# A hybrid block in one launch: two pairs of stages joined, expert weights kept in SBUF, residual rows loaded through ScalarE's queue

## The chip, the cores and the metric

The kernel runs on one core of a Trainium2 chip. The metric is the device time of one execution in microseconds, the median of several. The profile is of one execution.

## The reference

The input x has 2 x 2048 rows of 256 features. Four layers follow, each added to x:

```python
x = x + attn_a(layernorm(x), ...)   # neural memory
x = x + ffn(layernorm(x), ...)      # product-key memory
x = x + attn_b(layernorm(x), ...)   # causal attention, 16 heads of 16
x = x + ffn(layernorm(x), ...)      # the same weights again
```

The neural memory computes the gradients of a two-layer network over all rows, takes one step with them and reads the new network: `silu(q @ W0n.T) @ W1n.T @ Wout.T`. The ffn normalises its input a second time, by the mean and the variance of each feature over all rows, so every row must have been normalised before its first score can be made. It scores each row against keys, picks 8 of 4096 experts for each of 8 heads, and sums `gelu(x . w_down) * softmax * w_up` over them. All is float32.

## The kernel before

The program is a row of stages (`hybrid_block`, L2249). Each stage is one block with a hand-written instruction list for each engine, ended by a barrier; what passes from one stage to the next lies in HBM (the arrays x1, x2, x3 for rows, xt for transposed rows, and wct, kin_t, kout_parts for the expert weights). Stages stand in groups (`StageSemaphores`): between two groups all semaphores of the group are cleared between two more barriers, and the new ones are set one by one; within a group they are not.

Tiles: P = 128 partitions, a chunk CH is 256 rows (16 chunks), a block BLK is 512 rows (8 blocks). Stages in order:

- `memory_prepare`, then `layer_norm_pass` (tag nm_ln): the rows are normalised, stored, transposed and stored again as xt.
- `memory_gradients` (tag mg, L914): 32 tiles of 128 rows in a software pipeline three deep. Beside it, one item a step, the expert weights are prepared: key_in is transposed and split in two float16 parts, key_out split likewise, and SyncE stores the parts (`kin_parts`, `kout_parts`) in HBM. The rings of working tiles have 8 buffers.
- `memory_update` (tag mu): first_w and second_w, the two weights of the reading network.
- `memory_read` (tag mr, L1306): for each chunk the product `p_pre` with first_w (8 matmul instructions), sigmoid on ScalarE, the hidden product on VectorE, `p_out` with second_w (8 instructions), the sum with the rows x on VectorE, and the store. SyncE loads the transposed rows (L1327) and the rows (L1330) and stores the sum (L1342). TensorE's order is the first product of the next chunk, then the second product of this one. The group of the memory ends here.
- `product_key_memory` (tags f1, f2; shown as f, L269): first `layer_norm_pass` (f_ln) reads the rows that the stage before stored, makes the row statistics (L179), normalises (L197), transposes on TensorE (L144), copies on ScalarE (L163), stores xt (L108) and counts feature statistics (L204). Its SyncE list also loads the expert weights: 4 loads of kin_t and 4 of kout, 1 MB each, and wct of 1 MB. A last step on VectorE (L321 to L330) gives scale and shift of each feature. Then `routed_experts` (L346) starts: scores, picks, routing and the expert products, chunk by chunk, over 16 chunks.
- attention: `attention_project` (ap), `attention_units` (at, L1736), `attention_output` (ao, L2064). The last loads the attention rows (L2089, two loads of 128 KB for a chunk, in pieces of 256 bytes), transposes them (4 instructions), copies on ScalarE, multiplies with W_o (8 instructions) and adds the rows x (L2178). Then comes the second `product_key_memory`.

Waits: an engine's list is executed in order. A tile that is used again waits for its last reader through a semaphore; for instance in `memory_read` the first product waits for its load and for the hidden product two chunks before.

Of the kernel before, what the change touches and what calls it, by code (L numbers as in the profile page):

```python
# [50 lines left out]

LNB = 4
# [3 lines left out]
def layer_norm_pass(nc, sem, tag, x_dram, xt_dram, ident_dram, feature_stats=None, xln_dram=None,  # L56
                    prefetch=None, last_loads=None, last_root=None, last_statistics=None):
# [4 lines left out]
    with ExitStack() as ctx:  # L62
# [35 lines left out]
        def _(sp):  # L98
# [3 lines left out]
            def stores(b, u):  # L102
                if xln_dram is not None:
                    sp.dma_start(xln_dram.rearrange("(n p) d -> p n d", p=P)[:, bass.ds(b * BT, BT), :],
                                 xln[u % 2][:]).then_inc(xln_stored[u % 2], 16)
# [8 lines left out]
            with sp.Fori(0, n_it - 1) as i:  # L114
                for u in range(LNB):
                    sp.wait_ge(xln_ready, ONE + i * LNB + u + 1)

                    load(i + 1, u)
                    stores(i * LNB + u, u)
                    if prefetch is not None:  # L120
                        prefetch(sp, 0, u)
            for u in range(LNB):
                sp.wait_ge(xln_ready, ONE + NBLK - LNB + u + 1)
                stores(NBLK - LNB + u, u)
                if last_loads is not None and u == 0:

                    sp.wait_ge(xt_stored[0], ONE + 16 * NK)
                    last_loads(sp)
                if prefetch is not None:
                    prefetch(sp, 1, u)  # L130
            for u in range(2):
                sp.wait_ge(xt_stored[u], ONE + 16 * NBLK // 2 * NK)
                if xln_dram is not None:
                    sp.wait_ge(xln_stored[u], ONE + 16 * NBLK // 2)
# [17 lines left out]
        def _(act):  # L152
# [4 lines left out]
            def copy_xt(b, u, k):  # L157
# [3 lines left out]
                if feature_stats is not None:  # L161
                    two_before(act, counted, b, u)
# [8 lines left out]
            if last_root is not None:  # L171
                last_root(act)

        @block.vector
        def _(dve):
# [15 lines left out]
            def normalise(b, u, k):  # L191

                two_before(dve, xt_ready, b, u)
                if xln_dram is not None:
                    dve.wait_ge(xln_stored[u % 2], ONE + k * 16)
# [11 lines left out]
            with dve.Fori(0, n_it) as i:  # L207
                chain = Chain(dve, steps, i * LN_LINKS)
                for u in range(LNB + 2):
# [10 lines left out]
                    if u >= 2 and feature_stats is not None:  # L220
                        count_features(b - 2, u - 2)
                assert chain.n == LN_LINKS
            if last_statistics is not None:

                dve.wait_ge(counted, ONE + NBLK)
                last_statistics(dve)
# [42 lines left out]
def product_key_memory(nc, sem, tag, x_dram, y_dram, xt_dram, ident_dram, wct_dram, kin_dram, kout_dram, gamma, beta):  # L269
# [3 lines left out]
    with ExitStack() as ctx:  # L273
# [3 lines left out]
        wct = sb("wct", [P, DH, NSUB])  # L277
        kin_t = sb("kin_t", [P, 2, DH, NE], F16)
        kout = sb("kout", [P, 2, NX, D], F16)
# [6 lines left out]
        weights_loaded, kout_loaded = sem(tag + "weights_loaded"), sem(tag + "kout_loaded")  # L286

        def load_weights(sp, turn, u):
            if turn == 0:
                k = slice(u * NE // LNB, (u + 1) * NE // LNB)  # L290
                sp.dma_start(kin_t[:, :, :, k].rearrange("p a h e -> p (a h) e"),
                             kin_dram[:, :, :, k].rearrange("p a h e -> p (a h) e")).then_inc(weights_loaded, 16)
            else:
                k = slice(u * NX // LNB, (u + 1) * NX // LNB)
                sp.dma_start(kout[:, :, k, :].rearrange("p a x d -> p a (x d)"),
                             kout_dram[:, :, k, :].rearrange("p a x d -> p a (x d)")).then_inc(kout_loaded, 16)
                if u == 0:
                    sp.dma_start(wct[:], wct_dram).then_inc(weights_loaded, 16)

        with ExitStack() as first:  # L300
# [3 lines left out]
            bn_st, bn_mv = fb("bn_st", [P, DH, NBLK, 6]), fb("bn_mv", [P, DH, 2])  # L304
            bn_var, bn_tmp, gb = fb("bn_var", [P, DH]), fb("bn_tmp", [P, DH]), fb("gb", [P, 2, DH])

# [3 lines left out]
            def load_first_chunk(sp):  # L310
                sp.dma_start(xt_in[:], xt_dram[0, :, :, :]).then_inc(xt_loaded, 16)
                sp.dma_start(ident[:], ident_dram).then_inc(consts_loaded, 16)

# [4 lines left out]
            def feature_scales(dve):  # L318
                chain = Chain(dve, bn_steps)
                for dh in range(DH):  # L320
                    chain.mark(nc.vector.bn_aggr(bn_mv[:, dh, :], bn_st[:, dh, :, :].rearrange("p b s -> p (b s)")))  # L321
# [10 lines left out]
            def load_ahead(sp, turn, u):  # L332
                load_weights(sp, turn, u)
                if (turn, u) == (0, 0):
                    with nc.allow_non_contiguous_dma(reason="512 scalars"):
                        sp.dma_start(gb[:, 0, :], gamma.rearrange("(h p) -> p h", p=P)).then_inc(gb_loaded, 16)
                        sp.dma_start(gb[:, 1, :], beta.rearrange("(h p) -> p h", p=P)).then_inc(gb_loaded, 16)

            layer_norm_pass(nc, sem, tag + "ln_", x_dram, xt_dram, ident_dram, bn_st, prefetch=load_ahead,
                            last_loads=load_first_chunk, last_root=feature_root, last_statistics=feature_scales)  # L340

        routed_experts(nc, sem, tag, x_dram, y_dram, xt_dram, ident, xt_in, wct, kin_t, kout, scale, shift,
                       consts_loaded, xt_loaded, weights_loaded, kout_loaded, hidden)


def routed_experts(nc, sem, tag, x_dram, y_dram, xt_dram, ident, xt_in, wct, kin_t, kout, scale, shift, consts_loaded,  # L346
                   xt_loaded, weights_loaded, kout_loaded, hidden):


    with ExitStack() as ctx:  # L350
# [143 lines left out]
        def _(pe):  # L494
# [84 lines left out]
            pe.wait_ge(weights_loaded, ONE + 16 * (LNB + 1))  # L579
# [8 lines left out]
            pe.wait_ge(kout_loaded, ONE + 16 * LNB)  # L588
# [325 lines left out]
def memory_gradients(nc, sem, xln_dram, xt_dram, ident_dram, w, grad1, grad0t, experts):  # L914
# [3 lines left out]
    RING = 8  # L918
    w_q, keys, key_in, key_out, wct_dram, kin_dram, kout_dram = experts
    with ExitStack() as ctx:  # L920
# [11 lines left out]
        sig, a1, dsilu, err, d1 = ring("sig", [P, D]), ring("a1", [P, D]), ring("dsilu", [P, D]), ring("err", [P, D]), ring("d1", [P, D])  # L932
        tmp = ring("tmp", [P, D])
        a1t, errt = ring("a1t", [P, DH, P]), ring("errt", [P, DH, P])
# [4 lines left out]
        s = {n: sem("mg_" + n) for n in names}  # L939
        for n in ("xt_loaded", "xln_loaded"):  # L940
# [6 lines left out]
        keys_t, wct = sb("keys_t", [P, NH, NK, 2]), sb("wct", [P, DH, NSUB])  # L947
        kin, kin_parts = ring("kin", [P, XG, D], SLOTS), ring("kin_parts", [P, 2, XG * P], SLOTS, F16)
        kout, kout_parts = ring("kout", [P, XG, D], SLOTS), ring("kout_parts", [P, 2, XG, D], SLOTS, F16)
        p_prep = pb("prep")  # L950
        keys_loaded, prep_ready, prep_taken, kin_hi = (sem("mg_" + n) for n in ("keys_loaded", "prep_ready", "prep_taken", "kin_hi"))
        kout_hi, kout_lo, wct_stored = sem("mg_kout_hi"), sem("mg_kout_lo"), sem("mg_wct_stored")
        kin_loaded, kin_stored, kout_loaded, kout_stored = (
            [sem(f"mg_{n}{i}") for i in range(SLOTS)] for n in ("kin_loaded", "kin_stored", "kout_loaded", "kout_stored"))
# [13 lines left out]
        def pipeline(step):  # L968
            for n in range(NT + 3):
                step(n, n % RING)  # L970

# [3 lines left out]

        def kout_item(n):
# [1327 lines left out]
```

## Time and profile before

| | us |
|---|---|
| median of 3 runs | 3638.61 (3636.14 to 3642.56) |
| the profiled execution | 3640.09 |
| its span, first to last instruction | 3638.3 |
| TensorE busy | 3213.3 (88%) |
| VectorE busy | 2964.9 (81%) |
| ScalarE busy | 1570.6 (43%) |
| mean granted TensorE clock | 0.949 |

The span is measured from the first to the last instruction; 1.8 us of the execution lie around it. Stages by the timeline: gradients 75 to 281 us, update to 295.7, memory read to 361, first layer norm with feature statistics to 420, first expert stage to 1435, attention to 2564, of it the output stage from 2497; second layer norm to 2623, second expert stage to the end. The granted clock is a share of full speed: 1.00 is 2.4 GHz and 0.50 is 1.2 GHz. Busy shares are means over stages with different limits, so they don't tell what a change in one stage is worth.

### The profile page before, as it was taken

How to read it: one execution, taken by the hardware profiler on the slowest of the kernel's cores; microseconds unless marked ns; L12 is line 12 of the kernel's file. 1: busy time of each engine (PE TensorE's matmuls, PEld its weight loads, DVE VectorE, ACT ScalarE, POOL GpSimd, SP SyncE). 2: the span in 40 equal slices, each digit the busy share in tenths (PEclk: the TensorE clock that was granted, in tenths of full speed). 3: DMA queues.
4: the chain of work that ended last, by engine and by line, in shares of the span. 5: the costliest groups of instructions: out<-in, count | busy, mean ns of one | idle time of the engine just before them, and what ended most of it. 6: DMA issues, size and time to landing. Idle time of an engine off the chain costs nothing. (4 is left out here: it accounts for less than half of the span.)

```text
span 3638.3 us, 75919 instructions
## 1 busy us (share of the span) xinstructions
PE 3213.3 (88%) x29442; PEld 2250.7 (62%) x29442; DVE 2964.9 (81%) x8984; ACT 1570.6 (43%) x2146; POOL 676.2 (19%) x353
## 2 busy tenths in 40 slices
PE   3997579999999986789999999997379999999997
PEld 2886357778787875533333333334257787878786
DVE  5443799999999995788888888871599999999996
ACT  1221244444444441635666666664244444444441
POOL 0000023333333332010000000000023333333333
PEclk6999699999999998979999999998699999999999
DMA  5534600000000001851221212004600000000000
GB/s 180 194 101 142 206 7 10 19 10 19 10 19 10 19 8 42 228 90 27 44 48 32 38 29 47 7 6 116 233 10 10 14 16 16 13 19 10 19 7 16
DMA packets 203794, 190.52 MB, mean 52 GB/s; under 512 B 49910, under 2 KB 182326, under 8 KB 203062
## 3 DMA queue, kind: packets, MB, share of 16 engines
q1 hardware_dynamic: 201526, 184.22, 18.5%
q8 instruction: 230, 3.77, 0.4%
q10 hardware_dynamic: 1920, 1.57, 0.2%
q14 instruction: 118, 0.97, 0.1%
HBM read 121.05 MB, written 64.29 MB: 51 GB/s over the span
## 5 line engine op out<-in xcount | busy, mean ns | idle before, releaser
L521 PE MATMUL f_p_route<-f_x_w,f_y_hot 128*128 128x64 f16 x8192 | 897.3, 193 | 87.3 <-DVE f_weighted L793 76.0
L545 PE MATMUL f_p_out<-f_kout,f_hidden 128*128 128x256 f16 x6144 | 853.4, 273 | 17.9 <-POOL f_hidden L450 16.7
L534 PE MATMUL f_p_hid<-f_xtc,f_kin_t 128*128 128x256 f16 x6144 | 852.9, 273 | 4.8 <-ACT f_hidden L633 4.7
L450 POOL TENSOR_TENSOR f_hidden<-f_weighted,f_hidden 128x1024 f16<-128x1024 f32 x256 | 612.1, 2391 | 1278.1 <-DVE f_x_w L783 1273.7
L1999 DVE TENSOR_REDUCE at_part_max<-at_p_ring 128x1 f32<-128x512 f32 (+3 forms) x1280 | 706.2, 603 | 119.5 <-PE at_p_ring L1870 75.1
L521 PEld LDWEIGHTS f_p_route<-f_x_w,f_y_hot 128*128 128x128 f16 x8192 | 691.3, 98 | 136.4 <-issue 111.1
L545 PEld LDWEIGHTS f_p_out<-f_kout,f_hidden 128*128 128x128 f16 x6144 | 601.5, 98 | 196.8 <-issue 118.6
L1980 ACT ACTIVATE at_prob<-at_p_s 128x1024 f32<-128x1024 f32 (+3 forms) x640 | 546.5, 895 | 382.2 <-PE at_p_s L1916 190.7
L534 PEld LDWEIGHTS f_p_hid<-f_xtc,f_kin_t 128*128 128x128 f16 x6144 | 601.4, 98 | 77.9 <-issue 10.2
L638 ACT CAST f_hidden<-f_weighted 128x1024 f16<-128x1024 f32 x256 | 343.3, 1341 | 580.7 <-DVE f_weighted L793 580.7
L633 ACT ACTIVATE f_hidden<-f_p_hid 128x512 f32<-128x512 f32 x512 | 301.5, 595 | 438.5 <-PE f_p_hid L534 437.8
L1870 PE MATMUL at_p_ring<-at_k,at_q 96*128 96x512 bf16 (+3 forms) x1280 | 417.5, 364 | 44.5 <-DMA at_q<-qk 15.7
L1916 PE MATMUL at_p_s<-at_q,at_k 99*128 99x512 bf16 (+3 forms) x1280 | 360.5, 354 | 6.6 <-DMA at_q<-at_m_rows 5.5
L1870 PEld LDWEIGHTS at_p_ring<-at_k,at_q 96*128 96x128 bf16 x1280 | 120.2, 98 | 389.2 <-DVE at_part_max L1999 263.1
L793 DVE TENSOR_TENSOR f_weighted<-f_hidden,f_p_route 128x1024 f32<-128x1024 f32 x256 | 310.3, 1212 | 8.4 <-PE f_p_route L521 7.8
L778 DVE TENSOR_TENSOR f_y_hot<-f_y_iota,f_yq 128x2048 f16<-128x2048 f16 x256 | 315.8, 1234 | 0.0
L783 DVE TENSOR_TENSOR f_x_w<-f_hot,f_shares 128x2048 f16<-128x2048 f16 x256 | 311.4, 1216 | 0.0
L1933 PE MATMUL at_p_o<-at_prob,at_v 128*17 128x512 f32 (+3 forms) x2560 | 300.7, 542 | 0.0
L502 PE MATMUL f_p_sim<-f_wct,f_xn 128*128 128x512 f32 x512 | 266.2, 610 | 31.3 <-ACT f_xn L601 26.3
L434 POOL IOTA f_rank_iota<- 128x64 uint16 x2 | 0.4, 213 | 1479.8 <-POOLq L62 1479.8
L717 DVE FIND_INDEX8 f_top_key<-f_top,f_sim 128x8 uint16<-128x64 f32 x1024 | 200.3, 218 | 0.0
L776 DVE TENSOR_TENSOR f_hot<-f_y_iota,f_xq 128x1024 f16<-128x1024 f16 x256 | 195.6, 764 | 1.1
(252 smaller groups left out, 3190.2 us busy)
## 6 DMA issues: line engine op xcount, KB each, us to landing
at_q<-qk SPq DMA_DIRECT2D x42, 256.0 KB, 4.6
at_k<-qk SPq DMA_DIRECT2D x42, 256.0 KB, 4.4
f_ln_xin<-x SPq DMA_DIRECT2D x16, 512.0 KB, 6.3
xt<-f_ln_xt SPq DMA_DIRECT2D x32, 256.0 KB, 6.0
f_kin_t<-kin_t SPq DMA_DIRECT2D x8, 1024.0 KB, 8.5
f_xt_in<-xt SPq DMA_DIRECT2D x32, 256.0 KB, 2.9
f_kout<-kout_parts SPq DMA_DIRECT2D x8, 1024.0 KB, 8.1
f_xres<-x SPq DMA_DIRECT2D x32, 256.0 KB, 2.7
```

Source lines behind the costliest of these rows:

```text
L450: nc.gpsimd.tensor_tensor(lo, weighted[s % WR], hi, ALU.subtract).then_inc(lo_ready, 1)
L521: last = nc.tensor.matmul(p_route[:, t, :], y_hot[:, s % HR, t // PAIR, :, t % PAIR], x_w[:, s % HR, half, t // PAIR, :, t % PAIR], start= ...
L534: last = nc.tensor.matmul(p_hid[g % 2][:, xp % 2, :], kin_t[:, a, dh, xp * P:(xp + 1) * P], xt[slot][:, b, dh, :], start=i % 6 == 0, stop= ...
L545: last = nc.tensor.matmul(p_out[:, u, :], parts[slot][:, xp, u * P:(u + 1) * P, a], kout[:, b, xp, :], start=g == 0 and i == 0, stop=xp == ...
L638: nc.scalar.copy(hi, weighted[s % WR]).then_inc(hi_ready, 1)
L778: nc.vector.tensor_tensor(y_hot[:, s % HR, :, :, :], y_iota[:].unsqueeze(1).to_broadcast(tall), tokens(yq[slot], tall), ALU.is_equal)
L783: nc.vector.tensor_tensor(x_w[:, s % HR, :, :, :, :], hot[:].unsqueeze(1).to_broadcast(both), shares[slot][:, s, :, :].rearrange("p h (t k ...
L793: nc.vector.tensor_tensor(weighted[s % WR], h, p_route[:].rearrange("p t (u x) -> p x u t", u=2), ALU.mult).then_inc(routed, 1)
L1870: last = nc.tensor.matmul(bank[:, 0:cols], q[slot][0:KS_ROWS, h, qt * P:(qt + 1) * P], k[slot][0:KS_ROWS, h, kb * BLK:kb * BLK + cols], st ...
L1916: last = nc.tensor.matmul(p_s[pair][:, j, off:BLK], k[slot][0:KS_ROWS + M_ROWS, h, kt * P:(kt + 1) * P], q[slot][0:KS_ROWS + M_ROWS, h, qb ...
L1980: nc.scalar.activation(prob[g % 2][:, 2 * pair:2 * pair + 2, off:BLK], p_s[pair][:, :, off:BLK], ACT.Exp).then_inc(s["prob_ready"], 1)
L1999: nc.vector.reduce_max(part_max[qb][:, row, kb:kb + 1], one[:, 0:cols], axis=AX.X).then_inc(s["turn_taken"], 1)
```

## The change

1. `memory_read` and the layer norm of the first `product_key_memory` become one stage, and so do `attention_output` and the layer norm of the second. A new class `FeatureNorm` has, for each engine, the step that the layer norm takes after the work of chunk c (`vector_step`, `tensor_step`, `scalar_step`, `sync_step`). The sum is written to one of NY = 3 row buffers, from which it is both stored and normalised; the layer norm's loads of rows are gone. The loop runs over 16 + 4 steps, written out.
2. The joined stages now stand in the group of `product_key_memory`, so the end of a group, which stood between the two, stands ahead of both.
3. The expert weights (wct, kin_t, kout) have one place in SBUF from the gradients to the end. `memory_gradients` writes the parts there; their stores and all later loads are gone. Its working rings have 4 buffers instead of 8.
4. In the joined stages ScalarE issues the loads of the residual rows x (`load_x`), at the end of its step; each waits for the sum that frees its buffer. On SyncE the load of chunk c + 2 stands ahead of the store of chunk c.
5. The attention's rows are stored in (T, D) layout and loaded with one load for a chunk, in pieces of 1 KB. A tile `out_t` lies in second_w's place. The layer norm of the memory writes its transposed rows to an array of its own.

The core of the diff:

```diff
+    def vector_step(self, dve, chain, c):
+        if c % 2 == 0 and 0 <= c // 2 - 1 < NBLK:
+            self.normalise(dve, chain, c // 2 - 1)
+        if c % 2 and c // 2 < NBLK:
+            self.statistics(dve, chain, c // 2)
+        if c % 2 and 0 <= (c - 5) // 2 < NBLK:
+            self.count(dve, (c - 5) // 2)
+
+    def tensor_step(self, pe, c):
+        m = (c - 3) // 2
+        if c % 2 and 0 <= m < NBLK:
+            pe.wait_ge(self.xln_ready, ONE + m + 1)
+            if m >= 2:
+                pe.wait_ge(self.xt_copied, ONE + m - 1)
+            for t in range(BT):
+                for h in range(DH):
+                    last = self.nc.tensor.transpose(self.pxt[m % 2][:, h, t * P:(t + 1) * P],
+                                                    self.xln[m % 2][:, t, h * P:(h + 1) * P], self.ident[:])
+            last.then_inc(self.xt_ready, 1)
+
+    def scalar_step(self, act, c):
+        m = c // 2 - 1
+        if c % 2 == 0 and 0 <= m < NBLK:
+            act.wait_ge(self.var_ready, ONE + m + 1)
+            self.nc.scalar.activation(self.rstd[m % 2][:], self.var_eps[m % 2][:], ACT.Sqrt).then_inc(self.root_ready, 1)
+        m = c // 2 - 2
+        if c % 2 == 0 and 0 <= m < NBLK:
+            act.wait_ge(self.xt_ready, ONE + m + 1)
...
+            self.nc.scalar.copy(self.xt[m % 2], self.pxt[m % 2][:]).then_inc(self.xt_copied, 1)
+
+    def sync_step(self, sp, c):
+        m = (c - 5) // 2
+        if c % 2 and 0 <= m < NBLK:
+            sp.wait_ge(self.xt_copied, ONE + m + 1)
+            for k in range(BLK // CH):
+                sp.dma_start(self.xt_dram[m * (BLK // CH) + k, :, :, :],
+                             self.xt[m % 2][:, :, k * CH:(k + 1) * CH]).then_inc(self.xt_stored[m % 2], 16)
+        self.load_ahead(sp, c)
```

The lists of the joined memory read:

```diff
         @block.sync
+            def load_xt(c):
+                above(sp, pre_ready, c - 1)
+                sp.dma_start(xt[c % 2][:], xt_dram[c, :, :, :]).then_inc(xt_loaded[c % 2], 16)
+
+            for c in range(NCH + norm.LEAD - 1):
+                if c + 2 < NCH:
+                    load_xt(c + 2)
+                if c < NCH:
+                    norm.store_rows(sp, c, out_rows)
+                norm.sync_step(sp, c)
         @block.tensor
+            pre(0)
+            for c in range(NCH + norm.LEAD - 1):
+                if c + 1 < NCH:
+                    pre(c + 1)
+                if c < NCH:
+                    out(c)
+                norm.tensor_step(pe, c)
         @block.scalar
+            def load_x(c):
+                above(act, norm.y_ready, c - 1)
+                act.dma_start(x[c % 2][:], rows[:, c * 2:c * 2 + 2, :]).then_inc(x_loaded[c % 2], 16)
+            for c in range(NCH + norm.LEAD - 1):
+                if c + 1 < NCH:
+                    sigmoid(c + 1)
+                norm.scalar_step(act, c)
+                if c + 2 < NCH:
+                    load_x(c + 2)
         @block.vector
+            hidden(0)
+            for c in range(NCH + norm.LEAD - 1):
+                if c + 1 < NCH:
+                    hidden(c + 1)
+                if c < NCH:
+                    residual(c)
+                norm.vector_step(dve, chain, c)
```

`attention_output` has the same form, with `load_rows` for `load_xt`, `turn` (four transposes) for `pre`, `copy_rows` for `sigmoid`, `product` for `out`, and no hidden product. In the gradient stage:

```diff
-            def store_kin(i):
-                sp.wait_ge(prep_taken, ONE + FIRST_KIN + i + 1)
-                e0 = i // DH * XG * P
-                sp.dma_start(kin_dram[:, :, i % DH, e0:e0 + XG * P], kin_parts[i % SLOTS][:]).then_inc(kin_stored[i % SLOTS], 16)
...
-                    above(act, kin_stored[i % SLOTS], i // SLOTS * 16)
-                    nc.scalar.mul(kin_parts[i % SLOTS][:, 0, :], p_prep[:], E_SCALE).then_inc(kin_hi, 1)
+                    nc.scalar.mul(kin_home(i, 0), p_prep[:], E_SCALE).then_inc(kin_hi, 1)
...
-                    above(dve, s["grads_added"], n - RING + 1)
+                    above(dve, s["grads_added"], n - WORK + 1)
```

## Rows read from the trace of the kernel before

**Rows 1.** Busy time of stretches: window, its length, each engine, PEclk, DMA share, GB/s.
```profile
75.00:281.00 206.00, 198.78 (x1032) 174.96 (x1032) 86.28 (x188) 51.87 (x125) 0.00 (x0) 0.98 0.44 141
305.00:356.00 51.00, 50.91 (x236) 44.42 (x234) 20.67 (x31) 8.36 (x14) 0.00 (x0) 1.00 0.73 212
366.00:418.00 52.00, 15.74 (x64) 12.55 (x64) 44.23 (x179) 11.01 (x18) 0.00 (x0) 0.50 0.90 309
2508.00:2559.00 51.00, 38.81 (x179) 31.57 (x177) 11.07 (x16) 8.21 (x14) 0.00 (x0) 0.90 0.76 213
```

**Rows 2.** Timeline, memory read's start and end: start us, duration us, engine, line.
```profile
295.75 0.36 SPq L1327 DMA_DIRECT2D mr_xt<-xt  x1
...
309.32 0.69 DVE L1412 TENSOR_TENSOR mr_y<-mr_p_out,mr_x 128x512 f32<-128x512 f32 x1 [0.41 <-PE mr_p_out L1379]
...
355.94 0.69 DVE L1412 TENSOR_TENSOR mr_y<-mr_p_out,mr_x 128x512 f32<-128x512 f32 x1 [1.03 <-PE mr_p_out L1379]
...
362.02 2.03 SPq L100 DMA_DIRECT2D f_ln_xin<-x  x4
```

**Rows 3.** Timeline, the attention output's start, its second sum, and the second expert stage's start.
```profile
2494.82 0.38 SPq L1829 DMA_DIRECT2D attn_rows<-at_ao  x1
...
2497.28 0.35 SPq L2084 DMA_DIRECT2D ao_ident<-ident  x1
...
2510.96 0.69 DVE L2178 TENSOR_TENSOR ao_y<-ao_p_y,ao_x 128x512 f32<-128x512 f32 x1 [1.28 <-PE ao_p_y L2148]
...
2623.47 0.06 DVE L835 MEMSET f_tile_base<- 64x1 f32 x1 [3.01 <-PEq L62]
```

**Rows 4.** Timeline, one chunk of memory read in steady state.
```profile
321.21 1.89 PE L1379 MATMUL mr_p_out<-nm_second_w,mr_hid 128*128 128x256 f32 x8
321.31 0.40 SPq L1342 DMA_DIRECT2D x<-mr_y  x1
...
322.94 1.89 PE L1370 MATMUL mr_p_pre<-mr_xt,nm_first_w 128*128 128x256 f32 x8
323.14 0.69 DVE L1412 TENSOR_TENSOR mr_y<-mr_p_out,mr_x 128x512 f32<-128x512 f32 x1 [0.41 <-PE mr_p_out L1379]
```

**Rows 5.** Timeline, one block of the first layer norm with feature statistics.
```profile
375.20 1.40 DVE L179 BATCH_NORM_STATS2 f_ln_ln_stats<-f_ln_xin 128x6 f32<-128x256 f32 x4
...
377.18 1.29 DVE L204 BATCH_NORM_STATS2 f_bn_st<-f_ln_xt 128x512 f32 x2
...
378.39 1.23 SPq L108 DMA_DIRECT2D xt<-f_ln_xt  x2
...
380.67 1.40 DVE L179 BATCH_NORM_STATS2 f_ln_ln_stats<-f_ln_xin 128x6 f32<-128x256 f32 x4
```

**Rows 6.** DMA issues: tile, queue, operation, count, KB each, median us from issue to landing.
```profile
xt<-f_ln_xt SPq DMA_DIRECT2D x32, 256.0 KB, 6.0
...
xt<-nm_ln_xt SPq DMA_DIRECT2D x16, 256.0 KB, 2.8
...
mr_xt<-xt SPq DMA_DIRECT2D x16, 256.0 KB, 3.6
```

**Rows 7.** Timeline, VectorE at the end of the first layer norm with feature statistics.
```profile
405.27 1.40 DVE L179 BATCH_NORM_STATS2 f_ln_ln_stats<-f_ln_xin 128x6 f32<-128x256 f32 x4
...
417.79 0.16 DVE L330 TENSOR_TENSOR f_shift<-f_gb,f_bn_tmp 128x2 f32<-128x2 f32 x1
...
420.31 0.06 DVE L835 MEMSET f_tile_base<- 64x1 f32 x1 [2.36 <-PEq L62]
```

**Rows 8.** Timeline, ScalarE's table loads in the layer norm and in an expert stage.
```profile
389.30 1.28 ACT L155 ACT_TABLE_LOAD   x1
...
392.67 0.20 ACT L155 ACTIVATE f_ln_rstd<-f_ln_var_eps 128x4 f32<-128x4 f32 x1 [2.08 <-DVE f_ln_var_eps L185]
...
483.14 1.28 ACT L618 ACT_TABLE_LOAD   x1
484.43 0.31 ACT L618 ACTIVATE f_expo<-f_expo 128x128 f32<-128x128 f32 x1
```

More of the change, by code:

```diff
@@ L2099, in finish @@
-            def finish(u, i, last=False):
-                sp.wait_ge(y_ready[u], ONE + i + 1)
-                if not last:
-                    load_x(u, i + 1)
-                sp.dma_start(yout[:, bass.ds(i * 4 + u * 2, 2), :], y[u][:]).then_inc(y_stored[u], 16)
-            def step(i, first, second):
-                next_rows(1, i, *first)
-                finish(0, i)
-                next_rows(0, i + 1, *second)
-                finish(1, i)
-            for u in range(2):
-                load_rows(u, 0, 0)
-                load_x(u, 0)
@@ L2142, in product @@
-            def product(u, i):
-                pe.wait_ge(copied[u], ONE + i + 1)
-                pe.wait_ge(y_ready[u], ONE + i)
+                        last = nc.tensor.transpose(p_t[u][:, h, t * P:(t + 1) * P], rows[u][:, t, h * P:(h + 1) * P], norm.ident[:])
+                last.then_inc(turned, 1)
+            def product(c):
+                u = c % 2
+                pe.wait_ge(copied, ONE + c + 1)
+                above(pe, norm.y_ready, c - 1)
                 for t in range(2):
@@ L2163, in _, with load_x @@
+            norm.wait_ident(pe)
+            turn(0)
+            pe.wait_ge(wo_loaded, ONE + 16)
+            for c in range(NCH + norm.LEAD - 1):
+                if c + 1 < NCH:
+                    turn(c + 1)
+                if c < NCH:
+                    product(c)
+                norm.tensor_step(pe, c)
         @block.scalar
         def _(act):
-            with act.Fori(0, BATCH * n_it) as i:
-                for u in range(2):
-                    act.wait_ge(turned[u], ONE + i + 1)
-                    act.wait_ge(summed[u], ONE + i)
-                    nc.scalar.copy(rows_t[u][:], p_t[u][:]).then_inc(copied[u], 1)
+            def load_x(c):
+                above(act, norm.y_ready, c - 1)
+                act.dma_start(x[c % 2][:], xin[:, c * 2:c * 2 + 2, :]).then_inc(x_loaded[c % 2], 16)
@@ new lines, in copy_rows @@
+            def copy_rows(c):
+                act.wait_ge(turned, ONE + c + 1)
+                above(act, summed, c - 1)
+                nc.scalar.copy(rows_t[c % 2][:], p_t[c % 2][:]).then_inc(copied, 1)
+            load_x(0)
+            load_x(1)
+            copy_rows(0)
+            for c in range(NCH + norm.LEAD - 1):
+                if c + 1 < NCH:
+                    copy_rows(c + 1)
+                norm.scalar_step(act, c)
+                if c + 2 < NCH:
+                    load_x(c + 2)
```

530 lines of the change are left out of this document (251 added, 279 removed).

## The prediction

> **What bounds the kernel now.** I read the table by stage first. The two expert stages (some 1,000 us each) and the attention products are the same instructions before and after; what the change reshapes is some 250 us in four short stages. The gradient stage is TensorE's: 198.8 busy of 206 us. Memory read is TensorE's too (50.9 of 51 us), at the full granted clock; the attention output shows 38.8 of 51, at 0.90. Both layer-norm stages with feature statistics are the opposite: TensorE 15.7 of 52 us, granted clock 0.50, while VectorE is busy 44.2 [rows 1]. So in each pair of neighbours one engine works while the other idles, and a barrier lies between.
>
> The timeline then gives the price of the seams. Memory read starts 0.3 us after the stage before it, but from its last sum (355.94 + 0.69 = 356.6) to the first layer-norm load there are 5.4 us, since that seam waits for a store and also closes a group of semaphores. A seam inside a group, from the last attention store (2494.82) to the next load (2497.28), takes 2.5 [rows 2, 3]. The group thus costs 5.4 - 2.5 = 2.9 us more; I use 2.9.
>
> **What a pair of chunks costs.** The joined loop treats two chunks of 256 tokens as one layer-norm block, so I count in pairs.
> TensorE: a product of eight instructions has a pitch of 322.94 - 321.21 = 1.73 us; four make 6.9 in memory read. The eight transposes take about 2 at half clock (estimate from their share of the 15.7 us in eight blocks), 1 at full: 7.9 in all.
> VectorE: one layer-norm block is 380.67 - 375.20 = 5.5 us in steady state: row statistics 2.0, feature statistics 1.3, the reciprocal and normalising the rest [rows 5]. To it come four passes of 0.69 in memory read (the hidden product and the sum, twice): 8.2; in the attention output two, 6.9. So neither bound alone gives the period; VectorE's is the lower limit.
>
> **The chain that I expect to set the period.** Let R(c) be the end of the sum of chunk c, c odd. On SyncE behind R(c) stand: its wait (0.1), the store of the rows (0.4), then two stores of transposed rows (1.2), and only then the load for chunk c+3 [rows 4, 5]. It is issued at R(c) + 1.7 and lands L later. TensorE's queue has the first product of c+3 ahead of the second product of c+2, so R(c+2) waits for that load: 0.1 + 1.73 (first product) + 1.93 (second product to the sum's start, 321.21 to 323.14) + 0.69 [rows 4]. The period is L + 6.15 us.
> L is unknown. Nearest rows: loads of the same tile land in 3.6 us; stores of this size in the first layer norm in 2.8; the same stores beside the 1 MB weight loads in 6.0 [rows 6]. The weight loads go away, but the new load stands behind three stores and beside ScalarE's load, so I take 4.0, near 3.6, and keep 2.8 and 6.0 as ends. Period 10.15.
>
> **Stage one (memory read and layer norm).** Its first loads are issued 2.9 us later than now, since the group closes ahead of it; so R(1) moves from 309.32 + 0.69 = 310.0 to 312.9 [rows 2]. Then come seven pairs: two without transposed stores yet (8.95 each), four of 10.15, and a last one with no load to wait for, at VectorE's 8.2: 66.7. R(15) is 379.6. Behind it come the same last steps as now: from the last row statistics (405.27) to the last shift (417.95) 12.7 us. The seam behind them is 2.4 us now, because SyncE waits for a transposed store among the weight loads; I expect VectorE to end last then, 0.4 [rows 7]. End 392.7 for 420.3 now: 27.6 us saved. ScalarE's row loads are issued beside this at 0.4 each and needed a pair later: nothing, while the cover of 8 us holds; without it, their landing would take L's place.
>
> **Stage two (attention output and layer norm).** The same chain, with 0.5 for the four transposes of rows instead of the first product: L + 4.9 = 8.9. TensorE would be busy 5.3 of it, less than in the attention output now, where the granted clock was 0.90; a fifth of the time at half speed doubles the 2.4 us of TensorE work in the chain, + 0.4 (an estimate): 9.25, and 8.05 without transposed stores. The start gains 1.3, since the rows are now the first load and not the third, and loses 2.9 to the group: R(1) from 2511.65 to 2513.2 [rows 3]. Seven pairs: 2 x 8.05 + 4 x 9.25 + 6.9 = 60.0; R(15) 2573.2; with the same 12.7 + 0.4, 2586.3 for 2623.5 now: 37.2 us saved. One load of 1 KB pieces for two with 256-byte pieces lies within L.
>
> **What I cost at nothing.** The weights' stores and 18 weight loads of 1 MB: the gradient stage is TensorE's in every step and waits for no store, and in the layer norm VectorE's steady 5.5 us waits for no load. They are hidden now; what they do cost, the late seam, is counted. The rings cut from 8 to 4: the wait for the gradients of tile n - 4 comes after a product that TensorE issues behind them, so it is already met. If it were not, each of 28 tiles would wait. The new row order of the attention rows: no store is waited for before the end. The expert stages start as now.
>
> **ScalarE's tables.** This speaks against the change. Sigmoid and square root now alternate, two table switches a pair, 16 in all, at 1.28 us. ScalarE's queue in an even step: square root, copy 1.0, wait for R(c+1), load 0.4, table 1.28, sigmoid 0.6, then hidden product. From R(c) on that gives the hidden product at about 8.1, where the chain above asks for it at about 8.8, if the table is loaded ahead of the sigmoid's wait, as the load at 389.30 was, 3.4 us ahead of its activation [rows 8]. Cost nothing, margin 0.7. If it stands behind the wait for the first product: 1.7 + 4.0 + 0.1 + 1.93 + 1.28 + 0.6 + 0.69 + 0.69 = 11.0, 0.85 more a pair.
> The rows show an activation starting 0.01 us behind a load of 1.28 us (483.14 + 1.28 to 484.43) [rows 8]. The Trainium skill, "ScalarE: Activation LUTs", What ACT_TABLE_LOAD costs, adds a drain of about 1380 ns to each load's 1283. By that rule, as an estimate from the page, both switches would cost 2.8 us more a pair and the total would lie 5 to 14 us higher; the trace does not agree.
>
> **Sum.** 27.6 + 37.2 = 64.8 us. The profiled execution took 3640.1 (span 3638.3); 3640.1 - 64.8 = 3575.3. The median is 1.5 below that execution: 3574. One us of L is worth 12.
>
> **The rivals.**
> *VectorE is the bound* (0.16): the loads come early enough, as the 2.8 us landings suggest. Stage one 2 x 6.9 + 5 x 8.2 = 54.8, stage two 2 x 5.6 + 5 x 6.9 = 45.7: 26 us better, 3548. Against it: SyncE issues in order, and the load is behind three stores.
> *The tables set stage one* (0.12): six pairs at 0.85 more, 3579.
> *Landings of 6.0* (0.11), as beside the weights: 12 x 2, 3598. For it: the joined loops move 2 MB in 9 to 10 us, somewhat more than the 212 GB/s of memory read [rows 1].
> *Slower* (0.03): landing alone decides. At L = 9.5 the gain of 65 is gone (5.5 x 12); the worst landing of these stores is near that, and at L = 10 the time would be 3646. Against: such landings were seen only beside weight loads.
> *No change* (0.02), 3639: the engines take turns in full. But even then a pair costs 6.9 + 5.5 = 12.4 and 12.0, which still saves some 35; it takes two such faults.
> The skill's drain is part of the tables' case (0.02 of it).
> My forecast, the SyncE chain, has 0.56, own range 3560 to 3588.
>
> **How the numbers follow.** Predicted 3574. The range goes from 3550 (most of VectorE's case) to 3598 (landings of 6.0). Faster by over 0.2% (7 us, about what this measurement tells from none): 0.95; within it 0.02; slower 0.03.
>
> **What the profile would show.** Right: one stage of about 95 us from 298 on, sums of odd chunks 10 us apart, TensorE waiting for the load of transposed rows and VectorE for the second product, clock near 1 in stage one; the second stage some 87 us. Wrong if: VectorE shows no idle time (its bound), the hidden product waits for the sigmoid behind a table load (tables), or the loads land later than 5 us. A gradient stage longer than 206 us, or expert stages that differ by over 2 us, would mean that I costed the weights' home or the shorter rings wrongly.

## The result and the profile after

The changed kernel takes 3581.35 us (median of 4 runs, 3579.15 to 3583.09), the kernel before 3639.86 in the same session; the ratio is 0.9838, with a 95% interval of 0.9823 to 0.9853. So 58.5 us are gone, where 64.8 were forecast (3574 us). The profiled execution has a span of 3578.7 us.

Busy time of three stretches of the changed kernel (columns as in [rows 1]): gradients, first joined stage, second joined stage.

```profile
75.00:281.00 206.00, 198.63 (x1032) 174.85 (x1032) 86.30 (x189) 51.91 (x125) 0.00 (x0) 0.98 0.31 95
305.00:380.00 75.00, 65.06 (x306) 53.94 (x304) 56.13 (x177) 33.09 (x42) 0.00 (x0) 0.97 0.59 190
...
2484.00:2550.00 66.00, 47.52 (x232) 38.59 (x231) 44.78 (x159) 16.14 (x28) 0.00 (x0) 0.90 0.67 211
```

The gradient stage is as before, with 95 GB/s instead of 141: the stores are gone and nothing else moved. In the joined stages TensorE and VectorE now work at the same time, but neither is full: TensorE 65 of 75 and 48 of 66 us, VectorE 56 of 75 and 45 of 66. Both wait. Who waits for what, in stage one and then in stage two (total us, times, longest us):

```profile
DVE mr_hid L1489 <- ACT mr_sig L1470: 21.2, 11, 10.9
...
PE mr_p_pre L1436 <- DMA mr_xt<-xt: 8.7, 9, 1.9
DVE f_ln_y L1495 <- PE mr_p_out L1447: 5.4, 11, 1.5
...
DVE f_ln_y L2249 <- PE ao_p_y L2205: 32.5, 8, 14.3
...
PE ao_p_t L2195 <- DMA ao_rows<-attn_rows: 16.0, 8, 3.3
```

TensorE waits for the load, in nearly every pair. VectorE waits for TensorE, in stage one also for the sigmoid, which itself waits for TensorE's first product (10.9 of its 21.2 us are one wait). One pair of stage one, in the timeline, shows the whole chain:

```profile
330.49 0.69 DVE L1495 TENSOR_TENSOR f_ln_y<-mr_p_out,mr_x 128x512 f32<-128x512 f32 x1
331.21 0.36 SPq L292 DMA_DIRECT2D x<-f_ln_y  x1
331.61 1.21 SPq L370 DMA_DIRECT2D xt<-f_ln_xt  x2
...
332.87 0.67 SPq L1414 DMA_DIRECT2D mr_xt<-xt  x1
...
336.59 1.99 PE L1436 MATMUL mr_p_pre<-mr_xt,first_w 128*128 128x256 f32 x8 [1.20 <-DMA mr_xt<-xt]
336.73 1.28 ACT L1470 ACT_TABLE_LOAD   x1
338.42 1.89 PE L1447 MATMUL mr_p_out<-second_w,mr_hid 128*128 128x256 f32 x8
338.62 0.60 ACT L1470 ACTIVATE mr_sig<-mr_p_pre 128x512 f32<-128x512 f32 x1 [0.60 <-PE mr_p_pre L1436]
...
340.35 0.69 DVE L1495 TENSOR_TENSOR f_ln_y<-mr_p_out,mr_x 128x512 f32<-128x512 f32 x1 [0.40 <-PE mr_p_out L1447]
```

The sum of an odd chunk ends at 331.18. SyncE issues its store, the two stores of transposed rows, and the load 1.69 us later. TensorE starts the first product 3.72 later, the second 1.83 later, the sum starts 1.93 after that and takes 0.69: 9.86 for the pair, where the prediction had 10.15 with a landing of 4.0. The table for the sigmoid is loaded while its input is still being computed.

The same in stage two, where TensorE waited longer:

```profile
2514.16 0.69 SPq L2172 DMA_DIRECT2D ao_rows<-attn_rows  x1
...
2517.92 0.88 PE L2195 MATMUL ao_p_t<-f_ident,ao_rows 128*128 128x128 f32 x4 [3.13 <-DMA ao_rows<-attn_rows]
2518.59 3.39 PE L2205 MATMUL ao_p_y<-ao_wo,ao_rows_t 128*128 128x256 f32 x8
...
2522.02 0.69 DVE L2249 TENSOR_TENSOR f_ln_y<-ao_p_y,ao_x 128x512 f32<-128x512 f32 x1 [3.41 <-PE ao_p_y L2205]
```

After the wait of 3.13 us the product took 3.39 us; in the pair before it, 1.89. The granted clock shows the cause. Over the whole stretch it is 0.90, but over the 4.1 us of this turn and product it is 0.58, close to the lower of the two levels, 1.2 GHz:

```profile
2517.90:2522.00 4.10, 4.08 (x14) 3.36 (x15) 0.71 (x3) 0.59 (x1) 0.00 (x0) 0.58 0.46 154
```

The seven pairs of stage two take 8.9, 7.1, 8.7, 10.2, 10.2, 10.4 and 6.7 us. The slow product stands in the three of over 10 us; in the pair of 8.7 TensorE waited 2.2 us for its load and the product behind it took 1.89.

The seams, which answer to [rows 2, 3, 7]:

```profile
296.78 0.95 ACTq L1464 DMA_DIRECT2D mr_x<-in_L_attn_a_x  x2
298.81 0.84 SPq L1414 DMA_DIRECT2D mr_xt<-xt  x2
...
392.03 0.16 DVE L441 TENSOR_TENSOR f_shift<-f_gb,f_bn_tmp 128x2 f32<-128x2 f32 x1
392.76 0.06 DVE L938 MEMSET f_tile_base<- 64x1 f32 x1 [0.57 <-PEq L1392]
...
2470.67 0.37 SPq L1913 DMA_DIRECT2D attn_rows<-at_ao  x1
...
2475.80 0.36 SPq L2172 DMA_DIRECT2D ao_rows<-attn_rows  x1
```

The first load of stage one is issued at 298.81 instead of 295.75, 3.1 us later (forecast 2.9). The seam into the expert stage is 0.57 us. From the last attention store to the first load it is 5.1 us.

### The profile page after: what moved, and what is told of

Read it like the earlier page. It is cut to its first block and busy times, and to the rows that moved or that the text cites. A ratio compares the mean times of both kernels' runs of the same rounds, so it can differ in the third digit from the quotient of the medians.

```text
span 3578.7 us, 75155 instructions
## 1 busy us (share of the span) xinstructions
PE 3207.6 (90%) x29442; PEld 2244.6 (63%) x29442; DVE 2963.7 (83%) x8984; ACT 1582.9 (44%) x2156; POOL 676.7 (19%) x353
## 5 line engine op out<-in xcount | busy, mean ns | idle before, releaser
L650 PE MATMUL f_p_out<-kout_in,f_hidden 128*128 128x256 f16 x6144 | 856.0, 274 | 17.5 <-POOL f_hidden L555 16.1
L639 PE MATMUL f_p_hid<-f_xtc,kin_in 128*128 128x256 f16 x6144 | 854.9, 273 | 5.9 <-ACT f_hidden L736 5.8
L650 PEld LDWEIGHTS f_p_out<-kout_in,f_hidden 128*128 128x128 f16 x6144 | 602.0, 98 | 197.0 <-issue 118.6
L639 PEld LDWEIGHTS f_p_hid<-f_xtc,kin_in 128*128 128x128 f16 x6144 | 602.1, 98 | 79.5 <-issue 9.7
L896 DVE TENSOR_TENSOR f_weighted<-f_hidden,f_p_route 128x1024 f32<-128x1024 f32 x256 | 313.9, 1226 | 10.5 <-PE f_p_route L626 9.4
L607 PE MATMUL f_p_sim<-wct_in,f_xn 128*128 128x512 f32 x512 | 267.1, 612 | 27.7 <-ACT f_xn L704 22.5
```

The source lines that it names most:

```text
L639: last = nc.tensor.matmul(p_hid[g % 2][:, xp % 2, :], kin_t[:, a, dh, xp * P:(xp + 1) * P], xt[slot][:, b, dh, :], start=i % 6 == 0, stop= ...
L650: last = nc.tensor.matmul(p_out[:, u, :], parts[slot][:, xp, u * P:(u + 1) * P, a], kout[:, b, xp, :], start=g == 0 and i == 0, stop=xp == ...
L896: nc.vector.tensor_tensor(weighted[s % WR], h, p_route[:].rearrange("p t (u x) -> p x u t", u=2), ALU.mult).then_inc(routed, 1)
```

## The experiments

Each ratio is to the kernel before, run on the same chip, with its 95% interval. I compare the kernels with each other by their medians, and by R(15) - R(1), the time from the end of the second sum to the end of the last one in the profile: 66.0 us in stage one and 62.3 in stage two of the changed kernel.

**e1: the load ahead of the stores of transposed rows**

```diff
-                if c + 2 < NCH:
+                if c % 2 and c + 2 < NCH:
                     load_xt(c + 2)
                 if c < NCH:
                     norm.store_rows(sp, c, out_rows)
+                if c % 2 and c + 3 < NCH:
+                    load_xt(c + 3)
                 norm.sync_step(sp, c)
```

The same with `load_rows`; chunk 2 is loaded ahead of the loop.

> Against the changed kernel (3581.3 us), in both joined stages SyncE issues the load for chunk c+3 behind the store of the rows of chunk c and ahead of the two stores of transposed rows, no longer behind them. If the chain through SyncE's list sets the period, each of the four pairs with such stores and a later load (c = 5, 7, 9, 11) gets the 1.2 us of the two stores back: 8 x 1.2 = 9.6 us, 3572, with odd sums about 8.6 apart in stage one instead of 9.8. If VectorE or the table switches set the period, nothing changes: 3581. If the transfers share a full DMA bandwidth, so that a load issued earlier lands no earlier, also 3581, with the landing longer by 1.2.

Measured: 3567.97 us, ratio 0.980 (0.9787 to 0.9814), 13.4 us less than the changed kernel. R(15) - R(1) is 60.7 in stage one, 5.2 less for the 4.8 expected, and 52.9 in stage two, 9.4 less: there the clock came back as well.

```profile
340.08 0.69 DVE L1498 TENSOR_TENSOR f_ln_y<-mr_p_out,mr_x 128x512 f32<-128x512 f32 x1
340.80 0.36 SPq L292 DMA_DIRECT2D x<-f_ln_y  x1
341.20 0.47 SPq L1414 DMA_DIRECT2D mr_xt<-xt  x1
...
341.71 1.20 SPq L370 DMA_DIRECT2D xt<-f_ln_xt  x2
```

Busy time of its two joined stages:

```profile
305.00:375.00 70.00, 63.75 (x301) 53.05 (x300) 55.22 (x175) 33.08 (x42) 0.00 (x0) 0.98 0.65 203
2484.00:2538.00 54.00, 41.17 (x217) 32.36 (x217) 44.17 (x158) 15.62 (x28) 0.00 (x0) 0.97 0.83 258
```

The load now leaves 0.4 us behind the sum. Its landing did not grow (3.6 us median as before), although the DMAs carry 258 GB/s in stage two instead of 211. So full bandwidth was not the limit, and neither VectorE nor the tables set the period.

**e2: the load ahead of the sum**

```diff
+            load_xt(2)
             for c in range(NCH + norm.LEAD - 1):
-                if c + 2 < NCH:
-                    load_xt(c + 2)
+                if c + 3 < NCH:
+                    load_xt(c + 3)
```

> In both joined stages the load for chunk c+3 is issued ahead of the store of chunk c, so it waits for the first product of chunk c+1 alone and for no sum. The chain theory: the load leaves the chain. Stage one is then set by ScalarE's list behind the sum of the even chunk (row load 0.46, table 1.28, sigmoid 0.60, hidden product 0.69, sum 0.69) at about 8.6 us a pair, or by VectorE at 8.2: R(15) - R(1) from 66.0 to 55 or 57. Stage two by VectorE at 6.9: from 62.3 to about 46. Sum -26: 3555. Rival, VectorE sets the period already: 3581. Rival, bandwidth: the joined loops move 190 to 211 GB/s, and if that is the limit the loads only wait longer: 3575 to 3581.

Measured: 3553.15 us, ratio 0.9762 (0.9749 to 0.9775); 28.2 us less than the changed kernel, forecast 26. R(15) - R(1): 55.6 and 45.7. Busy time:

```profile
330.00:366.00 36.00, 34.66 (x173) 29.30 (x171) 33.94 (x113) 21.43 (x27) 0.00 (x0) 1.00 0.78 248
2496.00:2524.00 28.00, 22.77 (x135) 19.39 (x134) 26.86 (x95) 9.93 (x17) 0.00 (x0) 1.00 0.94 302
```

VectorE is at 94 and 96% of these stretches, the clock is full, and a pair takes 8.23 us in stage one and 6.74 in stage two, near the prediction's bounds of VectorE, 8.2 and 6.9. In stage one TensorE is as busy as VectorE (96%; the prediction had 7.9 a pair for it), and 0.2 to 0.3 of the 8.23 are a wait for the sigmoid:

```profile
342.92 1.28 ACT L1471 ACT_TABLE_LOAD   x1 [0.58 <-DVE f_ln_y L1496]
344.22 0.60 ACT L1471 ACTIVATE mr_sig<-mr_p_pre 128x512 f32<-128x512 f32 x1
...
344.85 0.69 DVE L1490 TENSOR_TENSOR mr_hid<-mr_p_pre,mr_sig 128x512 f32<-128x512 f32 x1 [0.22 <-ACT mr_sig L1471]
```

Without that wait a pair takes 7.94 us (e7 and e8 below); in that stretch no wait of VectorE is left there, and TensorE waits for VectorE. With the same double buffers, the whole distance between the forecast's case and the VectorE rival is one place in SyncE's list.

**e3: the stores of transposed rows issued twice**

```diff
-            for k in range(BLK // CH):
+            for xt_dram in (self.spare, self.xt_dram):
+                for k in range(BLK // CH):
```

> Each store of transposed rows is issued twice, the first time to a spare array that nobody reads. The output is unchanged. Chain theory: 1.2 us more between the sum and the load in four pairs of each stage, +9.6 and perhaps as much again from longer landings: 3591 to 3596. VectorE or the tables as the bound: less than 3 us, because the chain would have room: 3581 to 3584.

Measured: 3613.02 us, ratio 0.9929 (0.9915 to 0.9942): 31.7 us more than the changed kernel. The direction was as expected, the size three times my 9.6 and beyond the 15 that I allowed for.

```profile
374.27 0.36 SPq L293 DMA_DIRECT2D x<-f_ln_y  x1
374.67 2.02 SPq L372 DMA_DIRECT2D f_spare<-f_ln_xt  x2
376.73 1.29 SPq L372 DMA_DIRECT2D xt<-f_ln_xt  x2
...
378.07 0.62 SPq L1416 DMA_DIRECT2D mr_xt<-xt  x1
...
383.69 3.78 PE L1438 MATMUL mr_p_pre<-mr_xt,first_w 128*128 128x256 f32 x8 [5.85 <-DMA mr_xt<-xt]
387.27 3.19 PE L1449 MATMUL mr_p_out<-second_w,mr_hid 128*128 128x256 f32 x8
```

In this pair, the longest, three things add up: the issue of the stores (2.02 + 1.29 for 1.2), the landing (5.6 for 3.7, behind 1 MB of stores), and the two products behind the wait at the lower clock (3.58 to the second one's start and 3.2 for 1.83 and 1.9). The granted clock from the first product's start to the end of the second (383.7 to 390.5 us) is 0.55. The slope of the chain is therefore not 1: here a longer wait also made the work behind it slower.

**e4: the residual rows on SyncE again** (part 4 undone)

```diff
                 if c < NCH:
                     norm.store_rows(sp, c, out_rows)
+                if c + 2 < NCH:
+                    load_x(c + 2)
                 norm.sync_step(sp, c)
```

> Part 4 of the change undone: SyncE issues the loads of the residual rows, behind the store of each chunk. Chain theory: 0.4 to 0.5 us more on SyncE between the odd sum and the load of chunk c+3 in six pairs of each stage: +5, 3586. Against it stands that ScalarE gets its 0.46 back behind each sum: if ScalarE's list (loads and tables) set stage one, this kernel would be faster than the changed one by some 3 us: 3578. VectorE as the bound: 3581.

Measured: 3585.59 us, ratio 0.9854 (0.9839 to 0.9869), 4.2 more, forecast 5; the two intervals overlap, so this difference by itself is a hint. R(15) - R(1) grows by 1.6 and 1.0, and the second sum of stage two comes 2.6 us later behind the last attention store, since the first loads queue up. So the 5 came out partly by luck: the two loops gave 2.6 of it and the start of stage two the rest, while in the totals of stage one a slow pair of the changed kernel (11.6 us, see below) hides part of the growth. Pair by pair the forecast of 0.4 to 0.5 holds: the 9.86 and 9.75 of stage one are 10.20 and 10.33 here. The kernel did not get faster, so ScalarE's list is not what sets the pace.

**e5: the weights' home alone**, the stages separate as before

> Part 3 (and the row order of the attention rows, part 5) of the change alone: memory read, attention output and both layer norms are stages of their own as before, with the group ends where they were; the gradient stage writes the expert weights to their SBUF home, and the layer norms' 18 weight loads of 1 MB are gone. By my prediction the stores and loads were hidden, and only the late seam ahead of each expert stage goes, 2.0 us each: 4 to 5 us less than the 3639.5 of before, 3635. Rival: the weight loads slowed the layer norms (they filled 0.90 of the DMA time), and much of the 58 us comes from them: under 3620. Rival: no difference, 3639.

The edit is long; its core in the layer norm of `product_key_memory` is

```diff
             def load_ahead(sp, turn, u):
-                load_weights(sp, turn, u)
                 if (turn, u) == (0, 0):
```

Measured: 3638.82 us, ratio 0.9999 (0.9990 to 1.0008). Nothing, where 4 to 5 us were expected. The layer norm and its last step with the seam:

```profile
366.00:418.00 52.00, 15.73 (x64) 12.54 (x64) 43.33 (x177) 11.00 (x18) 0.00 (x0) 0.50 0.47 146
```

```profile
417.32 0.16 DVE L446 TENSOR_TENSOR f_shift<-f_gb,f_bn_tmp 128x2 f32<-128x2 f32 x1
418.04 0.06 DVE L948 MEMSET f_tile_base<- 64x1 f32 x1 [0.56 <-PEq L64]
```

The DMA share falls from 0.90 to 0.47, and the layer norm is not faster: the 18 MB were hidden, as the prediction said. The late seam is gone (0.56 us, 2.36 in [rows 7]), also as it said. But it is worth less than 2.0 us: from the last sum of memory read to the expert stage it takes 62.2 us, for 63.5 to 63.7 in three profiles of before (e10 and e11 give two of them), and from the last sum of the attention output 62.4, for 63.8 to 64.6. That is 2.6 to 3.7 us for both seams where 4 to 5 were expected, and the interval allows a gain of up to 3.6. So the runs do not settle whether a small gain is there or the long stages gave it back; e10 and e11 look into the long stages.

**e6 and e7: no table switches in stage one**, on the changed kernel and on e2

```diff
-            ...activation(self.rstd[m % 2][:], self.var_eps[m % 2][:], ACT.Sqrt)
+            ...activation(self.rstd[m % 2][:], self.var_eps[m % 2][:], self.root)
```

with `self.root` the sigmoid in stage one.

> In stage one the root of the row variances is taken with the sigmoid function instead of the square root (the rows are then normalised with a wrong factor), so the 16 switches of ScalarE's table are gone; the other stages are unchanged. By the chain through SyncE: nothing, 3581. If the tables held the period: 0.85 us or more for each of six pairs, 3576 or less; by the skill's drain of some 1380 ns a load (Trainium skill, ScalarE: Activation LUTs, What ACT_TABLE_LOAD costs), an estimate from the page, up to 14 us less, 3567.

Measured: 3579.51 us, ratio 0.9844 (0.9829 to 0.9858), the changed kernel's. R(15) - R(1) in stage one is 66.1 for 66.0. The 16 switches cost nothing there.

> The same edit on top of e2, where VectorE works without a gap but for 0.2 us a pair behind the sigmoid whose table is loaded behind a row load (e2's rows, 342.92 + 1.28 to the hidden product at 344.85). So 0.2 x 7 = 1.5 us less than e2's 3553.2: 3552. If the switches cost their 1.28 us in this faster loop: 7 x 1.28 = 9 us less, 3544.

Measured: 3551.59 us, ratio 0.976 (0.9746 to 0.9773), e2's within the interval. R(15) - R(1) in stage one is 53.8 for e2's 55.6, 1.8 us less for the 1.5 forecast; a pair takes 7.94 us for 8.23. Even where VectorE has next to no slack, the two switches of a pair, 1.28 us each, cost 0.3 us. The medians are too close to show this, and e8 shows that the switches do not cost it alone.

**e8: e2 with the residual rows on SyncE**

```diff
+                if c + 3 < NCH:
+                    load_xt(c + 3)
                 if c < NCH:
                     norm.store_rows(sp, c, out_rows)
+                if c + 2 < NCH:
+                    load_x(c + 2)
```

> e2 with the residual rows loaded by SyncE again, behind the store of each chunk. On the changed kernel this cost 4.3 us (e4), by the chain. In e2 no load waits behind a sum in SyncE's list until a pair later, so the chain theory expects 0 to 2 us (the first loads queue up at each stage's start): 3553 to 3555. If the cost was ScalarE's lighter list against SyncE's issue time in itself, the 4 us come again: 3557.

Measured: 3554.20 us, ratio 0.9765 (0.9751 to 0.9778), e2's. What part 4 is worth, it is worth through the chain of SyncE's list; with that gone, it can stand in either list. In stage one it stands even better on SyncE: a pair takes 7.95 us for e2's 8.23, as in e7, with the table switches still there. In e2 the sigmoid's table is loaded behind a row load that waits for the sum; without that row load it is loaded early enough. So the 0.3 us belong to the row load and the table together, and taking away either one gives them back. The median shows nothing of it, since the first expert stage was 2.8 us longer in e8's profile than in e2's.

**e9: one term of VectorE's bound moved** (e2, stage two)

```diff
+            for t in range(BT):
+                last = self.nc.scalar.activation(self.xln[m % 2][:, t, :], self.y[m % NY][:, t, :], ACT.Identity,
+                                                 bias=self.offset[m % 2][:, t:t + 1], scale=self.rstd[m % 2][:, t:t + 1])
```

> e2 with one more edit, in stage two alone: ScalarE normalises the rows (4 instructions of 128x256, as a multiply and add with one factor and one offset a row), VectorE makes the offset (one small instruction of about 0.2 us) and no longer the four of 1.38 us together. In e2 VectorE works 26.9 of 28 us in stage two and its odd sums are 6.74 apart. If VectorE is the bound there, 6.74 - 1.38 + 0.2 = 5.6 a pair, seven pairs: 8 us less than e2's 3553.2, 3545. Rival: the DMAs (0.94 of the time busy in stage two, 302 GB/s) become the bound at once: nothing, 3553.

Measured: 3560.78 us, ratio 0.9779 (0.9766 to 0.9792): 7.6 more than e2 by the medians, not 8 less. The intervals of e9 and e2 overlap, so the medians alone show only that nothing was gained; the loop shows a loss. VectorE is no longer the bound (20.5 of 28 us), nor are the DMAs (0.89 busy, for 0.94 in e2), but a pair takes 7.30 instead of 6.74, and R(15) - R(1) 50.1 instead of 45.7, 4.4 us more.

```profile
2500.37 0.16 DVE L318 SCALAR_TENSOR_TENSOR f_ln_offset<-f_ln_mv,f_ln_rstd 128x4 f32<-128x4 f32 x1
2500.57 1.58 ACT L365 ACTIVATE f_ln_xln<-f_ln_y,f_ln_offset,f_ln_rstd 128x256 f32<-128x256 f32 x3
...
2502.06 0.59 ACT L365 ACTIVATE f_ln_xln<-f_ln_y,f_ln_offset,f_ln_rstd 128x256 f32<-128x256 f32 x1
...
2502.70 1.09 PE L353 MATMUL f_ln_pxt<-f_ident,f_ln_xln 128*128 128x128 f32 x8 [1.88 <-ACT f_ln_xln L365]
2503.63 0.60 PE L2214 MATMUL ao_p_t<-f_ident,ao_rows 128*128 128x128 f32 x4
2504.07 1.89 PE L2224 MATMUL ao_p_y<-ao_wo,ao_rows_t 128*128 128x256 f32 x8
```

The four instructions take 2.08 us on ScalarE for 1.38 on VectorE, TensorE waits 1.88 us for them with the transposes, and the turn and the product of the next chunk stand behind those transposes. I had taken a busy engine's load away and looked at its sum alone, not at the way round: sum, reciprocal, normalising, transposes, product, sum.

**e10: the kernel before, its expert tiles at other SBUF addresses; e11: the kernel before again**

```diff
+        pad = [sb(f"pad{u}", [P, DH, D]) for u in range(2)]
         wct = sb("wct", [P, DH, NSUB])
```

> The kernel before with 4 KB a partition allocated ahead of the tiles of the expert stages and used by nobody, so that these tiles lie at the SBUF addresses that they have when the weights have their home. e5 lost its seam gain of 4 us somewhere in the long stages. If the place of the tiles in SBUF lengthens the expert stages, this kernel is 2 to 5 us slower than before: 3641 to 3644, with stages of 1014 to 1017 us. If it is something else, or chance, 3639.

> The kernel before, unchanged, for a second profile of its long stages. If their length scatters from execution to execution, the first expert stage is some other number than 1011.8 us, anywhere up to the 1016.6 seen in e4; if these stages really got longer by the change, it is 1011.8 again, the second one 1014.8, attention 1062.7. The time: 3639.

Measured: 3637.77 and 3637.78 us, ratios 0.9999 (0.9990 to 1.0008) and 0.9997 (0.9988 to 1.0007). The place in SBUF costs nothing that can be seen. The lengths of the long stages (in us; an expert stage runs from its first instruction on VectorE to the issue of its last store or the end, attention from there to the issue of its last store, stage two from there to the second expert stage; in before, stage two is the attention output and the layer norm):

| | expert stage 1 | attention | stage two | expert stage 2 |
|---|---|---|---|---|
| before, e10, e11 | 1011.8, 1011.5, 1011.5 | 1062.7, 1063.2, 1063.2 | 128.7, 123.2, 125.0 | 1014.8, 1018.7, 1017.0 |
| e5 | 1012.4 | 1066.3 | 124.2 | 1018.4 |
| after, e1, e2 | 1014.8, 1013.4, 1013.6 | 1063.1, 1066.2, 1066.6 | 92.6, 83.2, 77.1 | 1015.5, 1014.7, 1016.5 |
| e4, e8 | 1016.6, 1016.4 | 1063.2, 1063.2 | 96.2, 78.6 | 1015.2, 1015.7 |

The first expert stage is the same to 0.3 us in three profiles of before, and 2 to 5 us longer in every kernel with joined stages (e3, e6, e7 and e9 too: 1013.6 to 1014.7). Each of these kernels was profiled once, so it is not shown that the amount belongs to the build. The second expert stage scatters by 4 us, of before too, and so does attention (1062.7 to 1066.6). Stage two of before alone differs by 5.5 us between its three profiles.

## Why the prediction was right

**The chain** that sets the period was right, link by link: load 1.69 us behind the sum (forecast 1.7), TensorE waiting for it, two products and the sum in TensorE's order. e1 took the stores out of it, e2 the sum, e3 and e4 made it longer, and each moved the time in the direction of the chain. L was 3.7 for 4.0. R(15) of stage one was forecast to end at 379.6 and ended at 378.93 + 0.68 = 379.6; the stage ends at 392.76 for 392.7. That is closer than the steps deserve: R(1) came 0.7 later (313.6), normal pairs were shorter by 0.3 to 0.4, the last pair took 7.3 for 8.2, and one pair took 11.6, because TensorE waited and then worked at the lower clock (2.56 and 3.05 us for two products, granted clock 0.68).

**The clock in stage two** is the term whose size was wrong. The prediction spread "a fifth of the time at half speed" over the stage, + 0.4 a pair. But the lower clock falls on the product right behind the long wait, which is in the chain, and costs its whole 3.39 - 1.89 = 1.5 us: three pairs took 10.2 to 10.4 us for 9.25, and the fourth, with its product at full speed, 8.7. R(15) - R(1) was 62.3 for 60.0. The start was 1.3 us better than forecast (17.1 us from the last attention store to R(1), for 18.4), so the stage as a whole, 92.6 us for 91.5, is near by luck. e1 and e2 gave the clock back (0.97, 1.00) together with the wait.

**VectorE's bound** (8.2 and 6.9) was right to 0.3 us, as e2, e7 and e8 show (7.94 and 6.74), and rightly not the case here.

**The tables** cost nothing, as predicted, and by the mechanism predicted: loads hoisted ahead of the sigmoid's wait, a small margin (the load at 336.73 ends 0.6 us ahead of its sigmoid at 338.62, forecast 0.7). e7 shows the margin gone in e2: 0.3 us a pair, together with the row load ahead of the table. The rule of the Trainium skill that was weighed ("ScalarE: Activation LUTs", What ACT_TABLE_LOAD costs: a drain of about 1380 ns beside the load) would have given e6 up to 14 us less. e6's loop was no shorter (66.1 for 66.0 us), and its median lies within the changed kernel's interval.

**The weights' home** was right in the gradient stage and in the layer norm (e5); the late seam was gone, but worth 1.2 to 2.2 us for the 2.0 taken. What e5 and the table above correct is the sentence "The expert stages start as now", with a difference of 2 us named as the sign of an error: the first one is 3.0 us longer (1014.8 for 1011.8). The prediction put this at nothing. Its cause is open: neither the shifted tiles (e10, 1011.5) nor the weights' home alone (e5, 1012.4) have it.

**The sum.** Against the profile that the prediction started from, the changed kernel's span is 59.6 us shorter, for 64.8: stage one 27.6 (forecast 27.6), stage two 128.7 - 92.6 = 36.1 (forecast 37.2), first expert stage -3.0, attention -0.4, second expert stage -0.7. So most of what is missing lies in the long stages that were put at nothing. Against the second profile of before (e11, span 3637.1) the account of 58.4 us closes to 0.1 so: stage one 27.6; stage two 125.0 - 92.6 = 32.4; first expert stage -3.2; attention 0; second expert stage +1.5. Here stage two falls short by 4.8, because the attention output and layer norm of before took 3.7 us more in the first profile than in this one (and 5.5 more than in e10). The 37.2 us rested on the length of these stages in one execution.

## What to carry to other kernels

- When two stages are joined, write down for each load what stands ahead of it in its queue's list, stores that wait for a late result above all. Here moving the load ahead of three stores was worth 28 us with no further buffer, half of what the whole change had brought (58).
- A wait in front of TensorE can have a second price, the products behind it at the lower clock. It does not follow every wait: in e3 the product behind a wait of 3.35 us took 3.78 us, the one behind a wait of 3.55 us took 1.99. Put the extra on those products, not on the stage's mean.
- Before work is moved off the busiest engine, follow the loop through the new one. The sum of busy times said 8 us less; the loop as it ran was 4 us longer.
- Read the length of the stages to be changed from more than one profile. Stage two of before took 123.2 to 128.7 us in three of them.

## What the runs showed of the hardware

**A load that lands late in every fifth chunk.** The expert stages repeat a chunk every 59.7 us, but in each profile some chunks take 0.3 to 1.5 us more (once in e4 and once in e8 over 3 us). In the first expert stage of before and e11 these are above all the third and the eighth interval between sums, in the changed kernel, e1, e2 and e6 the fourth and the ninth. The changed kernel's landing (from issue, by DMA issues) in a slow chunk, 737 to 798 us, and in the next one, 798 to 857:

```profile
f_xt_in<-xt SPq DMA_DIRECT2D x1, 256.0 KB, 4.7
...
f_xt_in<-xt SPq DMA_DIRECT2D x1, 256.0 KB, 2.8
```

And who waits for it, in the timeline of both:

```profile
742.87 1.09 ACT L704 ACTIVATE f_xn<-f_xt_in,f_shift,f_scale 128x256 f32<-128x256 f32 x2 [3.82 <-DMA f_xt_in<-xt]
...
802.15 1.09 ACT L704 ACTIVATE f_xn<-f_xt_in,f_shift,f_scale 128x256 f32<-128x256 f32 x2 [1.94 <-DMA f_xt_in<-xt]
```

The load lands 1.9 us later, once in five chunks, while the DMAs are only 0.05 busy over the chunk. Which chunk it hits differs between builds of the joined and the separate stages and is the same for two executions of one build. That may account for part of the longer first expert stage: of the 3 us that the changed kernel has more than before, these intervals make about 2 (two at 61.2 for 60.4 and 60.6, two more at 60.0 for 59.7), and the rest lies in the fourteenth (43.6 for 42.3), which other profiles also have at either length. What recurs in this rhythm is not settled; no run isolated it.

**VectorE's instruction times differ between profiles.** The three large products of the expert stage took 1226 to 1247 ns in the changed kernel's profile and 1212 to 1233 before. That is not an effect of the tiles' new place: e1 to e3, with the same places, have `f_hot` at 760 to 765 ns, as before (764), where the changed kernel has 777. One profile cannot say whether it is a trait of this execution or of this build.
